# Trainium2, one core: terms of the shift summed ahead by GpSimd and VectorE, loads reordered, TensorE's code written out

## The reference, cut to what matters

```
value = xf @ vp_w.T + vp_b                       # per pixel, G = 8 groups of 8 channels
om = depthwise3x3(x) @ om_w.T + om_b             # per pixel, group and tap: 2 offsets, 1 mask
py = row + tap_y + off_y ; px = column + tap_x + off_x
sampled = bilinear(value, py, px)                # zero outside the image
out = einsum('nhwgk,nhwgkc->nhwgc', mask, sampled) @ op_w.T
x = x + out
```

## Time and profile before

| | |
|---|---|
| median of 3 runs | 3491.53 us (3486.46 to 3496.63) |
| the profiled execution | 3484.53 us, its span 3482.5 us |
| PE, PEld busy | 2797.9 us (80%), 2290.3 us (66%) |
| DVE, ACT, POOL busy | 1877.5 us (54%), 2010.5 us (58%), 1791.0 us (51%) |
| L1245 apply on PE | 1091.8 us busy, 297.4 us idle before it, 219.5 of them on `abuf` from the scratch |
| L1224 windows on PE | 610.8 us busy, 12.6 us idle before it |
| L1038, L1041 merge on POOL | 316.7 and 330.9 us busy |
| q1 (SP's queue) | 488.15 MB, its packets 54.3% of 16 engines' span |

### The profile page before, as it was taken

How to read it: one execution, slowest core, us unless ns; L and a number is a source line. 1 busy time by engine, 2 the same in 40 slices (tenths; PEclk the granted TensorE clock), 3 DMA queues, 4 the chain that set the end, 5 groups by cost and what they waited for, 6 DMA issues and landing times. The chain is left out here.

```text
span 3482.5 us, 117965 instructions
## 1 busy us (share of the span) xinstructions
PE 2797.9 (80%) x47624; PEld 2290.3 (66%) x47624; DVE 1877.5 (54%) x2922; ACT 2010.5 (58%) x4273; POOL 1791.0 (51%) x1450
## 2 busy tenths in 40 slices
PE   4888567778179989897988889798988989798993
PEld 2555345656167777776777777677767777677882
DVE  3554412211476656666565666666565666666651
ACT  1222123222278777676767767686767767676870
POOL 0000000000378677676767677676766777676860
PEclk9999879889589999999999999999999999999996
DMA  4555388886466666666576666657576666657662
GB/s 108 149 143 144 84 203 208 213 206 175 107 158 175 189 177 178 181 171 182 161 190 171 185 180 172 181 165 187 159 189 172 183 181 170 183 163 190 171 171 73
DMA packets 480109, 587.20 MB, mean 169 GB/s; under 512 B 178840, under 2 KB 424032, under 8 KB 479584
## 3 DMA queue, kind: packets, MB, share of 16 engines
q1 hardware_dynamic: 361312, 488.15, 54.3%
q10 hardware_dynamic: 118272, 91.76, 8.3%
HBM read 351.92 MB, written 201.14 MB: 159 GB/s over the span
## 5 line engine op out<-in xcount | busy, mean ns | idle before, releaser
L1245 PE MATMUL acc_p<-abuf,vbd 128*32 128x102 f32 (+7 forms) x27648 | 1091.8, 333 | 297.4 <-DMA abuf<-weight_scratch 219.5
L1245 PEld LDWEIGHTS acc_p<-abuf,vbd 128*32 128x32 f32 (+1 forms) x27648 | 919.0, 145 | 471.6 <-DMA abuf<-weight_scratch 161.7
L1079 ACT ACTIVATE dwt<-xp,wts 128x224 f32<-128x224 f32 x2016 | 798.8, 481 | 140.8 <-ACT wst L1102 102.5
L1024 POOL TENSOR_TENSOR dwt<-dwt 128x896 f32<-128x896 f32 x224 | 496.3, 2216 | 575.3 <-ACT dwt L1079 573.8
L164 PE MATMUL cv<-cin,wb 128*64 128x392 bf16 x6912 | 635.7, 348 | 147.3 <-DMA cin<-sg 147.3
L955 DVE TENSOR_TENSOR pr<-mh_p,ht 128x864 f32<-128x864 f32 x672 | 669.2, 1051 | 23.2
L164 PEld LDWEIGHTS cv<-cin,wb 128*64 128x64 bf16 x6912 | 443.4, 115 | 333.5 <-issue 95.9
L1224 PE MATMUL win_p<-pr,smat 128*128 128x160 f32 x4032 | 610.8, 306 | 12.6 <-POOL pr L1041 12.6
L1224 PEld LDWEIGHTS win_p<-pr,smat 128*128 128x128 f32 x4032 | 556.7, 191 | 33.2 <-POOL pr L1041 10.9
L962 DVE TENSOR_TENSOR y<-y,misc 128x224 f32 (+1 forms) x224 | 86.7, 387 | 833.2 <-PE misc L1173 833.2
L1166 PE MATMUL om_p<-wts,omin 64*64 64x216 f32 x3584 | 378.1, 350 | 6.3 <-POOL omin L1031 6.3
(11 more groups left out here) (137 smaller groups left out, 2584.0 us busy)
## 6 DMA issues: line engine op xcount, KB each, us to landing
abuf<-weight_scratch SPq DMA_DIRECT2D x1568, 120.0 KB, 2.7
weight_scratch<-wst ACTq DMA_DIRECT2D x224, 400.0 KB, 3.4
xt<-x SPq DMA_DIRECT2D x128, 392.0 KB, 8.3
rows_scratch<-vsb SPq DMA_DIRECT2D x224, 128.0 KB, 2.6
vbd<-rows_scratch SPq DMA_DIRECT2D x896, 32.0 KB, 2.4
cin<-sg SPq DMA_DIRECT2D x128, 203.0 KB, 3.5
x_scratch<-xt SPq DMA_DIRECT2D x64, 392.0 KB, 5.5
y<-x SPq DMA_DIRECT2D x128, 196.0 KB, 3.6
```

Source lines behind the costliest of these rows:

```text
L1024: pool.tensor_tensor(d[:, 0:4, :], d[:, 0:4, :], d[:, 4:8, :], ALU.add).then_inc(dw1_ok, 1)
L1079: ins = act.activation(dwt[:, j % 2, k, :].rearrange("p (r w) -> p r w", w=W), image[:, r:r + BR, k % 3:k % 3 + W], ACT.Identity, scale=dw ...
L1245: mm = pe.matmul(acc_p[32 * (2 * s + b):32 * (2 * s + b) + 32, 0:TN].rearrange("p (k w) -> p k w", w=W)[:, k0:k1 + 1, x0:x1], vbd[0:K, 1 - ...
```

## The change

- **`windows`: five matmuls instead of nine.** One per column `e` of the window. What was accumulated in PSUM is now added ahead in SBUF, by two new additions in POOL's `merge`: `cells(1, 1:3) += cells(2, 0:2)` and then `cells(1, 0:2) += cells(0, 1:3)`, each of 5 x 64 = 320 columns.
- **One addition of rows moves from POOL to DVE.** What was L1038 (576 columns, both inputs in SBUF) now stands at the end of DVE's `products`.
- **POOL merges first.** `merge(t+1)` stands ahead of `depthwise(t+4)`.
- **DVE sums pieces ahead of `read_misc`**, in steps 1, 2, 4 and 6.
- **SP loads pieces in steps 0, 1, 3 and 5, behind `read_weights`**, in 4 DMAs instead of 6, two of them over 128 partitions. A store is one DMA of 128 partitions instead of two.
- **ACT normalises in quarters**, each just ahead of the taps that need it, where it was one activation of 56 rows.
- **TensorE's code is written out for all 16 pairs**; the other engines keep their loops.

```
--- before.py
+++ after.py
-        LOAD_AT = (0, 1, 2, 4)
-        SUM_AT = (1, 2, 3, 5)
-        STATS_AT, GROUPS_AT, NORM_AT = 7, 8, 9
+        LOAD_AT = (0, 1, 3, 5)
+        SUM_AT = (1, 2, 4, 6)
+        STATS_AT, GROUPS_AT = 7, 8
+        NORM_ROWS = H // 4
...
+        def norm_needed(j):
+            return min(H - 1, BR * (j + 1)) // NORM_ROWS
...
+                    sp.dma_start(y[:, bass.ts(q % 2, 1), at].rearrange("p a f -> p (a f)"),
+                                 x.rearrange("(q s) c f -> q (s c) f", s=S)[bass.ts(q, 1), :, at].rearrange("a p f -> (a p) f")).then_inc(xl_in[k % 2], 16)
+                    sp.dma_start(x3h[:, k % 2, :],
+                                 x3_d.rearrange("(q s) c f -> q (s c) f", s=S)[bass.ts(q, 1), :, at].rearrange("a p f -> (a p) f")).then_inc(xl_in[k % 2], 16)
                     for s in range(S):
-                        sp.dma_start(y[64 * s:64 * s + 64, bass.ts(q % 2, 1), at].rearrange("p a f -> p (a f)"),
-                                     x[S * q + s, :, at]).then_inc(xl_in[k % 2], 16)
-                        sp.dma_start(x3h[64 * s:64 * s + 64, k % 2, :], x3_d[S * q + s, :, at]).then_inc(xl_in[k % 2], 16)
...
-                    if not last and j in LOAD_AT:
-                        load_piece(i + 1, LOAD_AT.index(j))
                     read_weights(i, j)
...
+                    if not last and j in LOAD_AT:
+                        load_piece(i + 1, LOAD_AT.index(j))
...
+                    rows = lambda at: pr[:, j % 2, at, :, :, :].rearrange("p k e x z -> p k (e x z)")
+                    dve.wait_ge(pr_ok, 3 * t + 2)
+                    dve.tensor_tensor(rows(slice(1, 3)), rows(slice(1, 3)), rows(slice(5, 11, 5)), ALU.add).then_inc(mg1_ok, 1)
...
-                    read_misc(phase(i, j), i + 1 if j == GROUPS_AT and not last else None,
-                              near(i, j, 4, first, last), near(i, j, -2, first, last))
                     if not last:
                         if j in SUM_AT:
                             sum_piece(i + 1, SUM_AT.index(j))
                         if j == STATS_AT:
                             channel_stats(i + 1)
+                    read_misc(phase(i, j), i + 1 if j == GROUPS_AT and not last else None,
+                              near(i, j, 4, first, last), near(i, j, -2, first, last))
...
-                    pool.wait_ge(pr_ok, 3 * t + 2)
-                    pool.tensor_tensor(rows(slice(1, 3)), rows(slice(1, 3)), rows(slice(5, 11, 5)), ALU.add).then_inc(mg1_ok, 1)
+                    cells = lambda e, at: pr[:, j % 2, 0:RT, e, at, :].rearrange("p k x z -> p k (x z)")
                     pool.wait_ge(pr_ok, 3 * t + 3)
                     pool.wait_ge(mg1_ok, t + 1)
-                    pool.tensor_tensor(rows(slice(2, 4)), rows(slice(2, 4)), rows(slice(8, 5, -2)), ALU.add).then_inc(mg_ok, 1)
+                    pool.tensor_tensor(rows(slice(2, 4)), rows(slice(2, 4)), rows(slice(8, 5, -2)), ALU.add).then_inc(mg2_ok, 1)
+                    pool.wait_ge(mg2_ok, t + 1)
+                    pool.tensor_tensor(cells(1, slice(1, 3)), cells(1, slice(1, 3)), cells(2, slice(0, 2)), ALU.add).then_inc(mg3_ok, 1)
+                    pool.wait_ge(mg3_ok, t + 1)
+                    pool.tensor_tensor(cells(1, slice(0, 2)), cells(1, slice(0, 2)), cells(0, slice(1, 3)), ALU.add).then_inc(mg_ok, 1)
 
                 def step(i, j, first, last):
+                    n = near(i, j, 1, first, last)
+                    if n:
+                        merge(*n)
                     n = near(i, j, 4, first, last)
                     if n:
                         depthwise(*n)
-                    n = near(i, j, 1, first, last)
-                    if n:
-                        merge(*n)
...
                 def taps(i, j):
+                    for m in range(4):
+                        if norm_needed(j) == m and (j == 0 or norm_needed(j - 1) < m):
+                            normalise(i, m)
...
                     for e in range(CT):
-                        terms = [(a, b) for a in range(3) for b in range(3) if 2 - (a + b - 2) == e]
+                        a, b = ((2, 2), (1, 2), (1, 1), (1, 0), (0, 0))[e]
                         to = BANK * (e // 3) + 160 * (e % 3)
-                        for n, (a, b) in enumerate(terms):
-                            mm = pe.matmul(win_p[:, to:to + 160], smat[:, e, :],
-                                           pr[:, j % 2, 0:RT, a, b, :].rearrange("p r (k g) -> p k r g", g=G),
-                                           start=n == 0, stop=n == len(terms) - 1)
+                        mm = pe.matmul(win_p[:, to:to + 160], smat[:, e, :],
+                                       pr[:, j % 2, 0:RT, a, b, :].rearrange("p r (k g) -> p k r g", g=G),
+                                       start=True, stop=True)
...
-                for j in range(NT):
-                    step(0, j, True, False)
-                with pe.Fori(1, pairs - 1) as i:
+                for i in range(pairs):
                     for j in range(NT):
-                        step(i, j, False, False)
-                for j in range(NT):
-                    step(pairs - 1, j, False, True)
+                        step(i, j, i == 0, i == pairs - 1)
```

More of the change, by code:

```diff
@@ L776, in l1_pass @@
         act_passed = sem("act_passed")
-        rows_ok = sem("rows_ok")
+        rows_ok, mg2_ok, mg3_ok = sem("rows_ok"), sem("mg2_ok"), sem("mg3_ok")
         w_out, a_in, v_out = ([sem(f"{n}{u}") for u in range(2)] for n in ("w_out", "a_in", "v_out"))
@@ L808, in load_piece @@
                     sp.sem_inc(passed)
-                    wait(sp, out_ok[k], 16 * S * (q - 1))
+                    wait(sp, out_ok[k], 16 * (q - 1))
                     sp.sem_inc(passed)
+                    sp.dma_start(y[:, bass.ts(q % 2, 1), at].rearrange("p a f -> p (a f)"),
+                                 x.rearrange("(q s) c f -> q (s c) f", s=S)[bass.ts(q, 1), :, at].rearrange("a p f -> (a p) f")).then_inc(xl_in[k % 2], 16)
+                    sp.dma_start(x3h[:, k % 2, :],
+                                 x3_d.rearrange("(q s) c f -> q (s c) f", s=S)[bass.ts(q, 1), :, at].rearrange("a p f -> (a p) f")).then_inc(xl_in[k % 2], 16)
                     for s in range(S):
-                        sp.dma_start(y[64 * s:64 * s + 64, bass.ts(q % 2, 1), at].rearrange("p a f -> p (a f)"),
-                                     x[S * q + s, :, at]).then_inc(xl_in[k % 2], 16)
-                        sp.dma_start(x3h[64 * s:64 * s + 64, k % 2, :], x3_d[S * q + s, :, at]).then_inc(xl_in[k % 2], 16)
                         sp.dma_start(l2h[64 * s:64 * s + CO, k % 2, :],
@@ L821, in store_piece @@
                     sp.sem_inc(passed)
-                    for s in range(S):
-                        sp.dma_start(out[S * q + s, :, at],
-                                     y[64 * s:64 * s + 64, bass.ts(q % 2, 1), at].rearrange("p a f -> p (a f)")).then_inc(out_ok[k], 16)
+                    sp.dma_start(out.rearrange("(q s) c f -> q (s c) f", s=S)[bass.ts(q, 1), :, at].rearrange("a p f -> (a p) f"),
+                                 y[:, bass.ts(q % 2, 1), at].rearrange("p a f -> p (a f)")).then_inc(out_ok[k], 16)
                 def read_weights(i, j):
@@ L885, in _ @@
                 for k in range(PIECES):
-                    sp.wait_ge(out_ok[k], 16 * S * pairs)
+                    sp.wait_ge(out_ok[k], 16 * pairs)
             @block.vector
@@ L892, in sum_piece @@
                     yk = y[:, bass.ts(q % 2, 1), at].rearrange("p a f -> p (a f)")
-                    dve.wait_ge(xl_in[k % 2], 6 * 16 * (PIECES // 2 * q + k // 2 + 1))
+                    dve.wait_ge(xl_in[k % 2], 4 * 16 * (PIECES // 2 * q + k // 2 + 1))
                     dve.scalar_tensor_tensor(out=yk, in0=yk, scalar=ab3[:, 1:2], in1=x3h[:, k % 2, :],
@@ L1013, in deviation @@
                     pool.wait_ge(vr3_ok, q + 1)
-                    wait(pool, xp_ok, q)
+                    wait(pool, xp_ok, 4 * q)
                     pool.tensor_tensor(g3[:, 2:3], g3[:, 1:2], eps[:, 0:1], ALU.add).then_inc(ep3_ok, 1)
@@ L1066, in _, with normalise @@
             def _(act):
-                def normalise(q):
+                def normalise(q, m):
                     act.wait_ge(nb3_ok, q + 1)
-                    wait(act, misc_ready, phase(q, 0) - 4)
-                    act.activation(image[:, 1:1 + H, 1:1 + W],
-                                   y[:, bass.ts(q % 2, 1), :].rearrange("p a (r w) -> p (a r) w", w=W),
+                    rows = slice(NORM_ROWS * m, NORM_ROWS * (m + 1))
+                    act.activation(image[:, 1 + NORM_ROWS * m:1 + NORM_ROWS * (m + 1), 1:1 + W],
+                                   y[:, bass.ts(q % 2, 1), :].rearrange("p a (r w) -> p (a r) w", w=W)[:, rows, :],
                                    ACT.Identity, scale=g3[:, 2:3], bias=g3[:, 3:4]).then_inc(xp_ok, 1)
                 def taps(i, j):
+                    for m in range(4):
```

(9 more changed lines are left out.)

## The result

| | before | after |
|---|---|---|
| median of 14 runs each | 3497.34 us (3486.32 to 3508.35) | 3526.7 us (3503.48 to 3539.91) |
| profiled execution, its span | 3484.53, 3482.5 us | 3525.74, 3523.9 us |
| ratio to before | | 1.0083, 95% interval 1.0065 to 1.0102 |

The change made the kernel 0.8% slower: 29 us by the medians. The forecast was a gain of 127 us, and its range ended at 3500.

A forecast was written before the change was run, and what follows sets the result against it. PE was taken to bound most steps, transfers the rest; afterwards GpSimd with locks at 9.4 us a step. 133.4 + 12 + 1 = 146 us a pair, 127 us saved, gave 3365 us; range 3130 to 3500.

The forecast's parts named there:

- Pieces on VectorE: VectorE's steps with a piece: 12.6 us against 9.4, some 3 us of data wait; 12 us a pair added.
- the slack of 3.4 us: Pipeline's spare time over two 9.4 us steps, less row term, merge 3.6, PE 3.7 and VectorE 8.1.
- The first and last pairs: Pairs outside the 13 summed: few waits before, change by a few us, counted as nothing.
- the quarters: ACT's normalisation in quarters: 8.23 plus some 0.3 us stays under 9.4; 2 us sooner at the start.
- The sum: Pair time: 133.4 + 12 + 1 = 146 us, 9.8 less than 155.8; 127 us over 13 pairs.
- GpSimd and locks: GpSimd's step: 8.4 us without locks, 0.65 and 0.36 for VectorE's locks, 9.4 us in all.
- PE: Five matmuls of nine save 1.2 us, step 8.4 us; the 6.0 us a turn go, adding nothing to the sum.
- SP: Piece loads behind the weights' reads delay nothing due; 15 us of weight waits a pair fall to about 1.
- the first: Rival: locks cost no more than today, VectorE fits GpSimd's waits; 3130 to 3135 us, chance 0.22.
- the second rival: VectorE and GpSimd block each other, waits of w per operation, passing 155.8 at w = 1.3 us; 3640 us, chance 0.13.
- The third: Rival: no gain, transfers are the true bound, a pair 155 us; 3480 us, chance 0.10.
- The slower side: Outcome slower than before, chance 0.14; the mutual blocking of VectorE and GpSimd was named as this side.

The follow-up runs named there:

- e2: Changed kernel with the four pieces summed one step later each (steps 2, 3, 5, 7): 3319.52 us, ratio 0.9516.
- e1: Changed kernel with GpSimd's depthwise sums ahead of its merge again: 3477.72 us, ratio 0.9961.
- e3: Changed kernel with both edits, depthwise sums ahead of the merge and pieces summed one step later: 3231.05 us, ratio 0.9259.
- e9: Changed kernel with depthwise sums first and pieces summed a step later, plus the row addition back on GpSimd: 3446.78 us, ratio 0.9871.
- e4: Kernel before, with loads behind the weights' reads (steps 0, 1, 3, 5), sums in steps 1, 2, 4, 6, and TensorE written out: 3574.63 us, ratio 1.0232.
- e5: Kernel before with loads behind the weights' reads, TensorE written out, and pieces summed in steps 2, 3, 5, 7: 3425.23 us, ratio 0.9817.
- e11: Changed kernel with depthwise sums first and pieces summed a step later, plus SyncE's code written out: 3215.23 us, ratio 0.921.
- e8: Changed kernel with depthwise sums first, pieces a step later, only the first of GpSimd's two cell additions, seven shift matmuls: 3247.32 us, ratio 0.93.

## Why the prediction was wrong, by its own steps

- **The step that failed first: the piece's data in "Pieces on VectorE".** I had the load land 15.9 us after the start of the step's windows and VectorE there at 12.5, and so 3 us of wait, in the first piece only. Measured for the first piece: 21.6 and 13.6, a wait of 8. Of the 5.7 us too little, 4.0 are the turn of SP's loop, which I had counted for PE only, and 2.3 the landing, 5.7 where I took 3.4 from the weights' write, a transfer of another size at another time (from 1606.0 to 1613.5 the 16 DMA engines are at least 80% busy); the issues themselves took 0.8 less. The third and fourth piece land about as I had it, and still cost 1.3 and 3.9 us: VectorE was not late there, as I had assumed. And I let the wait be swallowed by slack. At 14 us a pair (e2) it is the whole difference between gain and loss.
- **The step that failed second: the slack of 3.4 us, "the round row term, merge 3.6, PE 3.7, VectorE 8.1".** It left out the depthwise sum. I named it as queued behind the merge, and did not follow who waits for it: PE's offsets do, and the projected output stands behind them. With 6.1 us more, and merge 3.4, PE 2.6 and VectorE 7.5, the round is 19.6 us, two whole steps. So a step is 9.8 and not 9.4, and no piece is caught up. e1 and e3 show it: 49 and 88 us for nothing but the order of two blocks on POOL.
- **The first and last pairs, put at nothing.** Of the 41 us between the two executions 31 lie outside the 13 pairs of my sum, 17 of them in pair 14, which has pieces to wait for as the others have and took only 143.3 us before. The 5 us ahead of the pass say little: with the same first layer and the same start of the pass, the first values come at 940.5 us in the changed kernel and at 931.9 in e1 and e9. From the matmul of the statistics (L1167, before L1155) to the first values it is 3.5 us where it was 5.5, the 2 us that I had put on the quarters. Why the first pair takes 9 us more was not tried.
- **The sum.** 14 x 9.8 + 2 = 139 where I had 133.4; pieces and waits 18 where I had 13. The pieces' own work costs little: e2 has no such wait, and its 143.05 is 4 above 139.
- **GpSimd and locks: nearly right**, though only where it shows, in e3. In a step without a piece it is 9.27 us for 9.4, row term 0.75 for 0.75 (1.35 with its wait), new additions 0.86 to 0.89 for 0.87, the locks 0.72 and 0.38 for 0.65 and 0.36. Over a whole pair POOL has 134.2 us of its own and of locks, where I had 133.4; that they come so close is in part luck. The operations last 1.4 us a step longer than alone and not 1.0, since the pieces lock POOL as well, and the bare step is 8.2 for 8.4. e3 lies at 3231 us, below my 3365, since with the data there and the order of before it needs only 3.5 us more than that, where I gave 13.
- **PE: right in its own records, wrong in the sum's reading.** Shift matmuls 1.6 us a step (1.5), no "issue" at the turn. I gave the written-out code nothing; in e4 and e3 it is worth 29 and 34 us, since the other engines cover only part of the turn.
- **SP: the number was right, the reason wrong.** Waits for `abuf` fell to 12 us, but by PE's lateness: luck. Once PE is in time they are 160 to 175 us again (e3, e5), against 151.0 before. Moving the loads behind the reads did not cure them. The turn of SP's loop is a part of them (91.8 are left in e11); whether the rest is bytes or latency was not tried.
- **The rivals.** The price of the locks was neither the first nor the second rival's; L950 is at 1.62 us on average, w = 0.6 and not 1.3. The third came nearest by its time, 3480, and not by its mechanism. The slower side should have been the data that arrives late.
- **What stays open:** why e8 is no faster than e3, why the weights' waits stay, and what the larger loads and the quarters of the normalisation are worth by themselves. Both were in the changed kernel and in all its variants, and in none of those made from the kernel before. A load of 392 KB over 128 partitions landed in 3.7 us (median from its issue) where one of 196 KB over 64 took 3.6, so twice the bytes came in the same time.

## What to carry to other kernels

When a load is moved back in its queue, count from its new issue (loop turns of the issuing engine included) to the landing, and move its consumer by as many steps: a wait for data holds up everything behind it on its engine, and one line of constants was worth seven times the change's net effect. When two blocks on an engine swap, follow both results around the whole ring of engines; the slack is two steps less every block that lies in the ring, and a block that was beside it may now be in it. And a wait that disappears after a change may only be hidden by a later one.

## What the runs showed of the hardware

- **The turn of a hardware loop costs SP some 3.8 to 4.0 us** (1596.38 to 1600.34 in after), as it does PE 6.0; with the code written out the gap between the same two issues is 0.1 us.
- **The lock's net price** on POOL's next operation was 0.72 us for VectorE's 1.04 and 0.38 for its 0.75 in the seven steps of e3 without a piece, 0.7 and 0.5 of VectorE's operation; in each of them VectorE's arrives while POOL is inside one. Over all steps, pieces included, POOL's seven operations took 9.17 us a step (means between 1400 and 3000) where they are 7.74 alone, 1.4 more.
- **GpSimd's addition** of 320 columns takes 0.86 to 0.89 us, on the line between 224 (0.66) and 448 (1.15).
